# A 24-unit transformer kernel: each batch's recurrent layer moved inside the other batch's feed-forward unit, with the delta masks in the first unit

## The reference

```python
def ffn(x):                       # hidden size 1024
    return (silu(x @ w_gate.T) * (x @ w_up.T)) @ w_down.T

def recurrent(x):                 # RG-LRU
    xr, y = split(x @ W_xy.T)                         # 256 and 256 features
    xc = conv_b + sum(conv_w[i] * shift(xr, 3 - i) for i in range(4))
    gate_x = sigmoid(block_diag(xc, ig_w) + ig_b)
    log_a = -8 * sigmoid(block_diag(xc, ag_w) + ag_b) * softplus(a_param)
    a = exp(log_a)
    h = scan(a, xc * gate_x * sqrt(-expm1(2 * log_a)))    # h[t] = a[t] h[t-1] + in[t]
    return (gelu(y) * h) @ W_resid.T

x = x + 0.5 * ffn(layernorm(x))
x = x + recurrent(layernorm(x))
x = x + 0.5 * ffn(layernorm(x))           # the same weights again
x = x + 0.5 * moe1(layernorm(x))          # 8 experts; the weights of each are W plus a sparse delta
# moe1: weighted = softmax(expert_atom_weights) @ atoms * sigmoid(importance)  [8 x 2048],
#       added to W[e] at the 2048 places mask_idx (places that occur twice are summed)
...
```

## Time and profile before

| what | value |
|---|---|
| median of the runs | 1224.28 us (1220.64 to 1522.63, three runs) |
| the profiled execution, its span | 1237.2 us |
| granted clock of PE over the span | 0.969 |
| PE, DVE, ACT, POOL busy | 91 %, 67 %, 50 %, 45 % |

### The profile page before, as it was taken

How to read it: one execution, slowest core, us unless ns; L and a number is a source line. 1 busy time by engine, 2 the same in 40 slices (tenths; PEclk the granted TensorE clock), 3 DMA queues, 4 the chain that set the end, 5 groups by cost and what they waited for, 6 DMA issues and landing times.

```text
span 1237.2 us, 22024 instructions
## 1 busy us (share of the span) xinstructions
PE 1122.8 (91%) x6730; PEld 940.8 (76%) x6730; DVE 832.0 (67%) x2284; ACT 614.5 (50%) x1444; POOL 550.8 (45%) x662
## 2 busy tenths in 40 slices
PE   5887788999899989988889998998899998999997
PEld 4776457777677778877676777986799997899995
DVE  5477676778987855558867875556766665665666
ACT  2455745321122335457848756545455554555552
POOL 5466818743336443235524426323354442544431
PEclk9898799999989999999999999999999999999999
DMA  5125322230004023422102162343011110010101
GB/s 175 59 69 182 120 81 66 88 115 19 1 1 185 0 77 117 137 69 61 39 15 47 41 229 101 113 128 107 27 43 34 34 43 26 27 51 25 51 1 34
DMA packets 48468, 87.89 MB, mean 71 GB/s; under 512 B 9664, under 2 KB 28480, under 8 KB 47936
## 3 DMA queue, kind: packets, MB, share of 16 engines
q1 hardware_dynamic: 42400, 75.15, 19.2%
q0 software_dynamic: 3968, 8.85, 2.4%
q10 hardware_dynamic: 2016, 2.83, 0.7%
HBM read 61.24 MB, written 19.27 MB: 65 GB/s over the span
## 4 chain that ended last, share of the span: by engine, by line
PE 54%; DVE 19%; ACT 6%; issue 4%; POOL 2%; another core or an unknown queue 0%; SPq 0%; DMA 0%; DVEq 0%; POOLq 0%; ACTq 0%
PE ps L283 16%; PE ps L285 15%; PE ps L284 15%; DVE a_ptl L1898 4%; PE ps L1874 3%; DVE a_p L1833 2%; ACT a_pth L1890 2%; ACT a_p L1841 2%; PE ps L869 1%; DVE x L1587 1%; PE ps L888 1%; DVE stats L329 1%; DVE x L1050 1%; PE ps L1609 1%; PE ps L419 1%
## 5 line engine op out<-in xcount | busy, mean ns | idle before, releaser
L1859 POOL TENSOR_SCALAR a_p<-a_p,small 128x128 f32<-128x128 f32 (+3 forms) x256 | 132.7, 536 | 218.9 <-DVE small L1850 218.2
L1841 ACT ACTIVATE a_p<-a_p,small 128x128 f32<-128x128 f32 (+3 forms) x256 | 141.6, 554 | 79.2 <-DVE small L1833 77.5
L1898 DVE TENSOR_TENSOR a_ptl<-ps,a_pth 128x384 fp32r<-128x384 f32 (+1 forms) x192 | 106.7, 596 | 62.2 <-ACT a_pth L1890 62.0
L283 PE MATMUL ps<-xh,wh 128*128 128x512 f32 x304 | 124.9, 411 | 8.9 <-POOL wl L518 5.6
L284 PE MATMUL ps<-xl,wh 128*128 128x512 f32 x304 | 121.1, 398 | 0.0
L285 PE MATMUL ps<-xh,wl 128*128 128x512 f32 x304 | 121.0, 398 | 0.0
L1890 ACT ACTIVATE a_pth<-ps 128x384 fp32r<-128x384 f32 (+1 forms) x192 | 90.5, 523 | 59.5 <-PE ps L1874 58.9
L1833 DVE CUSTOM_DVE_ANT_0 a_p<-ps,maskrow 128x128 f32<-128x128 f32 (+3 forms) x256 | 111.7, 484 | 5.4 <-PE ps L285 2.5
L395 POOL TENSOR_TENSOR rstd<-veps,nhalf 128x4 f32<-128x4 f32 x24 | 26.0, 1085 | 182.6 <-DVE veps L339 182.6
L487 POOL TENSOR_TENSOR wl<-raw,wh 128x256 fp32r<-128x256 f32 (+1 forms) x64 | 89.0, 1390 | 5.3
L1874 PE MATMUL ps<-ident,a_p 128*128 128x128 f32 x640 | 84.9, 280 | 5.0 <-DVE a_kl L1898 2.1
(11 more groups left out here) (373 smaller groups left out, 3403.3 us busy)
## 6 DMA issues: line engine op xcount, KB each, us to landing
raw<-in_w SPq DMA_DIRECT2D x32, 384.0 KB
raw<-in_qk SPq DMA_DIRECT2D x16, 512.0 KB
raw<-moe_x SPq DMA_DIRECT2D x60, 128.0 KB
moe_y<-m_y SPq DMA_DIRECT2D x60, 128.0 KB
m_raw<-in_ex SPq DMA_DIRECT2D x8, 608.0 KB, 7.8
m_a<-in_ex SPq DMA_DIRECT2D x8, 608.0 KB, 5.4
raw<-in_v SPq DMA_DIRECT2D x16, 256.0 KB
moe_x<-drh SPq DMA_DIRECT2D x8, 480.0 KB
```

The source lines that it names most:

```text
L283: pe.matmul(o, l[0], r[0], start=start, stop=False, skip_group_check=True)
L1841: s.activation(p[:, par, P_AT[i]:P_AT[i + 1]], p[:, par, P_AT[i]:P_AT[i + 1]], ACT.Exp, bias=h_nmx[:, par, i:i + 1], scale=scale, accum_ou ...
L1859: g.tensor_scalar(pp, pp, h_inv[:, par, i:i + 1], 1.0, ALU.mult, ALU.mult).then_inc(sem("at_norm"), 1)
L1898: ins = v.tensor_tensor(dst, ps[:, bank, 0:cols], f32(hi), ALU.subtract)
```

## The change

The recurrent layer of batch 0 (unit 2) is worked off inside unit 1, that of batch 1 (unit 3) inside unit 4; the stage of its own is gone, and with it `pe_warm` in it. Its parts stand between the chunks: PE takes `rg_x`, `gates`, `y` and `out` between gate and up and down of the chunks 1 to 7, and the last two `down` stand behind `rg_out`; ACT and DVE take the rest, with the recurrent residual, and the statistics of the next unit, ahead of chunk 7. The recurrent weights come by ACT's queue in unit 0; ACT makes their high half, POOL their low half after the chunks 4 to 7. ACT's queue zeroes the delta table. The masks are all 2048 wide and there are no spare rows any more: 13 masks in unit 0, 3 in unit 1. Each of POOL's 16 scatters waits for the one before it to have landed; they stand between the chunks of units 1 and 4, and four of them ahead of unit 4's first splits. All four quarters stand in unit 5. The diff, cut:

```diff
-        DELTA_UNITS = (0, 1, 4, 5)
-        QUARTERS = ((4, 1), (4, 3), (4, 5), (5, 1))
-        EQ_SLOTS = [[0], [1, 2], [3, 4], [5, 6], [7, 8, 9], [10, 11, 12], [13, 14, 15]]
+        QUARTERS = ((5, 1), (5, 2), (5, 3), (5, 4))
+        EQ_MASK = {1: [0], 2: [1], 3: [2, 3], 4: [4, 5], 5: [6, 7, 8], 6: [9, 10], 7: [11, 12]}
+        EQ_SUM = {4: [0, 1, 2, 3], 5: [4, 5], 6: [6, 7, 8], 7: [9, 10]}
+        EQ_MASK_LATE = [13, 14], [15]
+        EQ_SUM_LATE = [11, 12, 13, 14, 15]
...
+        RG_OF = {1: 2, 4: 3}
...  pe_ffn
+            pe_ready(pe, u)
+            gate_up(0)
+            gate_up(1)
+            if u in RG_OF:
+                r = RG_OF[u]
+                if u == 1:
+                    pe_equal(pe, EQ_SUM_LATE)
+                down(0)
+                gate_up(2)
+                if u == 1:
+                    pe.wait_ge(sem("d_cmb"), 3)
+                pe_T(pe, r)
+                down(1)
+                pe_rg_x(pe, r)
+                gate_up(3)
+                down(2)
+                gate_up(4)
+                down(3)
+                pe_rg_gates(pe, r, 0)
+                gate_up(5)
+                down(4)
+                pe_rg_gates(pe, r, 1)
+                gate_up(6)
+                pe_rg_y(pe, r)
+                down(5)
+                gate_up(7)
+                pe_rg_out(pe, r)
+                down(6)
+                down(7)
+                pe_T(pe, 4 if u == 1 else 5)
...  dve_ffn
+            if u in RG_OF:
+                r, nxt = RG_OF[u], 4 if u == 1 else 5
+                if u == 1:
+                    dve_stats(v, r)
+                    chunk(0)
+                    dve_equal(v, EQ_MASK_LATE[0])
+                    chunk(1)
+                    dve_equal(v, EQ_MASK_LATE[1])
+                    dve_combined(v)
...
+                chunk(2)
+                dve_rg_pad(v, r)
+                dve_T(v, r)
+                dve_rg_conv(v, r, 0)
+                chunk(3)
+                dve_rg_conv_lo(v, r, 0)
+                dve_rg_conv(v, r, 1)
+                chunk(4)
+                dve_rg_conv_lo(v, r, 1)
+                chunk(5)
+                dve_rg_gate_input(v, r, 0)
+                dve_rg_gate_input(v, r, 1)
+                dve_rg_square(v, r, 0)
+                dve_rg_square(v, r, 1)
+                dve_rg_scan(v, r)
+                dve_rg_gated_lo(v, r)
+                chunk(6)
+                dve_residual(v, r, 1.0, [("rg_out", 2 * (r - 2) + 1), ("rg_out", 2 * (r - 2) + 2)], rg_o)
+                dve_stats(v, nxt)
+                chunk(7)
+                dve_residual(v, u, 0.5, ready)
+                dve_T(v, nxt)
+                dve_stats(v, 3 if u == 1 else 6)
...  act_delta
+            if u == 0 and j == 1:
+                s.dma_start(rg_wf[:, :], a["rglru"]).then_inc(sem("rg_w_in"), 16)
+            if u == 0 and 2 <= j <= 5:
+                act_zero(s, j - 2)
+            if u == 0 and 4 <= j <= 7:
+                act_rg_weights(s, j - 4)
...  pool_scatter
             for k in ks:
+                if k:
+                    g.wait_ge(sem("d_scattered"), 16 * k)
...  SP
-            sp_resident(sp, "rglru")
             sp_resident(sp, "wt")
-            sp_zero(sp)
             sp_zero_x(sp)
+            sp.dma_start(d_q3[:, :, :], a["weight3"]).then_inc(sem("d_in_q3"), 16)
             chunks(4)
...  POOL
+            for i in range(1, CH0 // 2):
+                for p in range(2):
+                    pool_chunks(g, 0, i, p)
+                    if i >= 2:
+                        pool_rg_weights(g, 2 * i + p - 4)
...
+            pool_resident(g, "wt")
+            pool_scatter(g, range(6, 10))
+            pre(4)
+            pool_ln(g, 4)
+            pool_ln(g, 3)
```

More of the change, by code:

```diff
@@ L314, in dr @@
             return drh[:, at:at + n], drl[:, at:at + n]
-        LN_AT = {u: u for u in range(N_UNITS)} | {20: 19, 19: 20}
+        LN_AT = {u: u for u in range(N_UNITS)} | {20: 19, 19: 20, 4: 3, 3: 4}
         def dve_stats(v, u, tiles=range(TT)):
@@ L634, in act_router, with gate_up @@
             s.activation(ex, dl, ACT.Exp).then_inc(sem("rt_exp"), 1)
-        def ffn_loop(eng, u, step, first, last):
-            n = CHUNKS[KIND[u]]
-            first()
-            if u in DELTA_UNITS:
-                for j in range(2, n - 2):
-                    step(j, j % 2)
-            else:
-                with eng.Fori(0, (n - 4) // 2) as i:
-                    for p in range(2):
-                        step(i * 2 + (2 + p), p)
-            last(n)
+        RG_OF = {1: 2, 4: 3}
         def pe_ffn(pe, u):
             b, f0, r0 = u % 2, FFN_AT[u], RAW0[u]
-            def gate_up(j, p, early=False):
+            def gate_up(j):
+                p = j % 2
                 pe.wait_ge(sem("w_gu"), f0 + 1 + j)
-                if not early:
+                if j >= 2:
                     pe.wait_ge(sem("ffn_silu"), f0 - 1 + j)
@@ new lines, in pe_rg_y, with pe_rg_out @@
+        def pe_rg_y(pe, r):
+            b = r - 2
+            for c in range(DC):
+                pe.wait_ge(sem("rg_sigm"), 4 * b + 2 + c + 1)
+                mm3c(pe, ps[:, c, :], [rc(k * 512 + (DC + c) * P, P) for k in range(DC)], [xT(b, k) for k in range(DC)])\
+                    .then_inc(sem("rg_xy"), 1)
+        def pe_rg_out(pe, r):
+            b = r - 2
+            pe.wait_ge(sem("rg_gelu"), DC * (b + 1))
+            pe.wait_ge(sem("rg_glo"), DC * (b + 1))
+            for t in range(TT):
+                last = mm3c(pe, rg_o(t), [(rg_ch[b][:, c, t * P:(t + 1) * P], rg_cl[b][:, c, t * P:(t + 1) * P])
+                                          for c in range(DC)], [rc(RG_WR + c * D, D) for c in range(DC)])
+                if t % 2:
+                    last.then_inc(sem("rg_out"), 1)
@@ new lines, in pe_rglru, with act_rg_x @@
+        def pe_rglru(pe, u):
+            return
+        def act_rg_x(s, r):
+            b = r - 2
+            s.wait_ge(sem("const_rgp"), 1)
+            s.wait_ge(sem("rg_pad"), b + 1)
+            for c in range(DC):
+                s.wait_ge(sem("rg_xy"), 4 * b + c + 1)
+                s.activation(rg_xp[b][:, c, 3:3 + T], ps[:, c, :], ACT.Copy).then_inc(sem("rg_x"), 1)
+                s.activation(rg_xc[b][:, c, :], ps[:, c, :], ACT.Identity, bias=rgp[:, c, 4:5], scale=rgp[:, c, 3:4])\
+                    .then_inc(sem("rg_tap"), 1)
@@ new lines, in act_rg_roots, with act_rg_gated_hi @@
+        def act_rg_roots(s, r):
+            b = r - 2
+            for c in range(DC):
+                s.wait_ge(sem("rg_m2"), DC * b + c + 1)
+                s.activation(rg_th[b][:, c, :], rg_th[b][:, c, :], ACT.Sqrt, scale=-1.0).then_inc(sem("rg_sqrt"), 1)
+        def act_rg_gated_hi(s, r):
+            b = r - 2
+            for c in range(DC):
+                s.wait_ge(sem("rg_g"), DC * b + c + 1)
+                s.activation(rg_ch[b][:, c, :], rg_gy[b][:, c, :], ACT.Copy).then_inc(sem("rg_ghi"), 1)
@@ new lines, in act_rglru, with dve_rg_pad, dve_rg_conv @@
+        def act_rglru(s, u):
+            return
+        def dve_rg_pad(v, r):
+            b = r - 2
+            v.wait_ge(sem("const_rgp"), 1)
+            if b == 0:
+                v.wait_ge(sem("d_zeroed"), 64)
+                v.wait_ge(sem("rg_wlo"), 4)
+            v.memset(rg_xp[b][:, :, 0:3], 0.0).then_inc(sem("rg_pad"), 1)
+            v.wait_ge(sem("rg_pad"), b + 1)
+        def dve_rg_conv(v, r, c):
+            b = r - 2
+            v.wait_ge(sem("rg_x"), DC * b + c + 1)
+            v.wait_ge(sem("rg_tap"), DC * b + c + 1)
+            for k in range(3):
+                if k:
+                    v.wait_ge(sem("rg_conv"), 6 * b + 3 * c + k)
+                v.scalar_tensor_tensor(out=rg_xc[b][:, c, :], in0=rg_xp[b][:, c, k:k + T], scalar=rgp[:, c, k:k + 1],
+                                       in1=rg_xc[b][:, c, :], op0=ALU.mult, op1=ALU.add).then_inc(sem("rg_conv"), 1)
@@ L2443, in pe_delta @@
                 last.then_inc(sem("d_delta"), 1)
-            if u == 1 and 1 <= j <= len(EQ_SLOTS):
-                o = ps[:, 0, 0:NK * 25].rearrange("p (m n) -> p m n", m=NK)
-                for k in EQ_SLOTS[j - 1]:
-                    pe.wait_ge(sem("d_eqs"), k + 1)
-                    for m in range(k, NK):
-                        last = pe.matmul(o[:, m, 0:24], d_eq[:, k % 3, m * P:(m + 1) * P], d_wb[:, k, 0:24],
-                                         start=(k == 0 and m == 0), stop=(k == NK - 1), skip_group_check=True)
-                    last.then_inc(sem("d_comb"), 1)
+            if u == 0 and j in EQ_SUM:
+                pe_equal(pe, EQ_SUM[j])
             if u == 5 and j == 6:
```

573 lines of the change are left out of this document (239 added, 334 removed).

## The result

The changed kernel takes 1260.06 us (median of 4 runs, 1259.02 to 1264.69) against 1222.46 us; the ratio is 1.0313, 95% interval [1.0279, 1.0347]: slower by some 38 us, where 17 were forecast. One of the four runs of before, of 1522.63 us, is left out of the ratio. The changed kernel's profiled execution has a span of 1258.3 us at a mean clock of 0.954.

The account below looks back on a forecast made before the run. The removed recurrent stage was taken as bound by waits on ACT and DVE. Units 0, 1, 4 and 5 at 70.7 + 75 + 68 + 48 = 261.7 against 245.1 gave +16.6 us, 1241; forecast 1229 to 1249, wider range 1206 to 1262.

Parts of the forecast that it names:

- the reference: Stages of units 0 to 5 in the first profile of before, 245.1 us; the difference was added to the median, 1224.3.
- the chain from `rg_x` to `rg_out`: Units 1 and 4: serial recurrent steps, mostly on ACT and DVE, with six table loads, 32.9 us in each unit.
- unit 1's tail: Unit 1 from `rg_out` to unit 4: `rg_out`, residual, statistics, chunk 7, last `down` and hand-off in series, 20.5 us.
- the start of `rg_x` in unit 4: Unit 4: `rg_x` comes at 14.7 us, as in unit 1 without masks, sums and one start at half clock.
- the price of nothing for four scatters: POOL ahead of unit 4's first splits: 9.7 us of scatters, beside unit 1's 20 us tail, costed at nothing.
- POOL's chain: Unit 0: POOL's split behind `rcl` sets chunk 4 to 5 (8.8 us) and 6 to 7 (8.0 us).
- unit 4's tail: Unit 4 from `rg_out` on, in series as in unit 1: 20.4 us.
- the half clock that the prediction adds there: Unit 0: `gate_up` behind long PE idle runs at half clock, 2.3 us added to each of two POOL chains.
- Rival 1: Units 0, 1, 4, 5: PE is the bound and waits are filled, 36 us less, 1188; chance in full 0.13.
- Rival 2: Units 0, 1, 4: half clock does not end, 16 to 20 us uncounted, 1257 to 1261; chance 0.22.
- Rival 4: Half the waits added in series fall together, 1209 to 1228; chance 0.17 together with half of rival 1.
- Rival 3: Chains in units 1 and 4: each table load also costs a drain of 1.38 us, 17 us more, 1258; chance 0.02.

Follow-up runs that it names:

- the run with the loads first: Changed kernel, recurrent weights' low halves out of unit 0, norm's pair of units 4 and 5 earlier, four unit 4 weight loads ahead of the zeroing: 1236.56 us, 1.0118.
- the run with the weights later: Changed kernel with the recurrent weights' low halves on POOL moved from unit 0's chunks to behind unit 2's layer norm in unit 1: 1254.18 us, 1.0270.
- The fillers: The run with the loads first plus 24 matmuls that compute nothing in PE's waits ahead of `rg_out` and the last `down`, units 1 and 4: 1235.89 us, 1.0113.
- narrow masks and mended queues: The run with the loads first, with masks 128 wide and one matmul of sums each: 1224.55 us, 1.0013 against the kernel before.
- the one with the quarters on POOL: The run with the loads first, with POOL instead of DVE making the low halves of unit 5's four quarters: 1234.61 us, 1.0125.

## Why the prediction was too small

The sign of the whole was right, the size was not: 17 us were forecast and 38 came. For units 1 and 4, the heart of the change, even the sign was wrong: the forecast took them to gain 11 us on the stages that they replace (143.0 against 154.3), and they lost 5. Of the 21 us between, the sum of the four stages was 14.8 too low and the reference 3.5 too high (245.1 against 241.7), which makes 34.9 by the stages; the other 2.7 of the 37.6 lie behind unit 5, where the profiles differ by more than that among themselves. The 14.8 are 6.7 of the chain from `rg_x` to `rg_out` in two units, 4.8 of unit 1's tail, 1.8 of the start of `rg_x` in unit 4 (16.5 for 14.7), 2.2 of unit 5, less 1.2 of unit 0, and 0.5 of the rest.

**The step that failed outright is the price of nothing for four scatters.** "The four ahead of unit 4's first splits take 4 × 2.4 = 9.7 us of POOL, beside the 20 us tail of unit 1 [...] so I cost them at nothing." They started at 140.3, only 10 us ahead of the time at which POOL was wanted, and took 14.1 us up to the end of the last, because each waited for a landing beside the 3.8 MB of zeros and the loads behind them. The tail took 25.3 us for 20.5 (the items given add up to 20.7), and 21.1 with the scatters out of the way: they cost 4.2 us of it. (The two other profiles that have scatters and norm's pair as the change put them show 25.0 and 24.3.) In the run with the loads first, where the scatters stand in the same place but the zeros come later and the norm's pair earlier, the tail from `rg_out` to unit 4 is 16.5 us (140.55 to 157.07), and with the weights later that run gives back 24 of the 38 us; the scatters alone, moved into unit 4, give nothing in all, for there PE waits 3.25 and 2.84 us for the splits behind them. The price of 2.4 us had come from a row without such a neighbour, and the neighbour stood in the diff.

**The chain from `rg_x` to `rg_out`** took 36.1 and 36.4 us for 32.9: over both units the largest term that was mis-sized. Its durations came from rows of the recurrent stage beside which POOL worked at the layer norm's small pair, at scatters or at nothing. Beside POOL's splits the same DVE steps are longer. In unit 1 (first three rows of the second block) the second convolution takes 3.38 where the first had 2.33, the scan pair 3.01 for 2.33, and the two products 1.95 for 1.26 (first block, of before); in unit 4 the convolution takes 3.38, the scan's inputs 2.17 for 1.28, and the scan pair 3.40.

```profile
161.41 1.26 DVE L1486 TENSOR_TENSOR rg_gy<-rg_gy,rg_xc 128x512 f32<-128x512 f32 x2
```

```profile
114.95 3.38 DVE L1504 SCALAR_TENSOR_TENSOR rg_xc<-rg_xp,rgp,rg_xc 128x512 f32<-128x512 f32 x3
...
135.83 3.01 DVE L1536 TENSOR_TENSOR_SCAN rg_xc<-rg_a,rg_xc 128x512 f32<-128x512 f32 x2
138.76 1.95 DVE L1541 TENSOR_TENSOR rg_gy<-rg_gy,rg_xc 128x512 f32<-128x512 f32 x2
...
192.82 3.38 DVE L1504 SCALAR_TENSOR_TENSOR rg_xc<-rg_xp,rgp,rg_xc 128x512 f32<-128x512 f32 x3
...
212.30 2.17 DVE L1532 TENSOR_TENSOR rg_xc<-rg_xc,rg_ga 128x512 f32<-128x512 f32 x2 [0.86 <-ACT rg_ga L1477]
214.39 3.40 DVE L1536 TENSOR_TENSOR_SCAN rg_xc<-rg_a,rg_xc 128x512 f32<-128x512 f32 x2
```

These steps are 2.4 us longer in unit 1 and 3.0 in unit 4, of the 3.2 and 3.5 by which the chain was too short. No run took the splits away from beside them. The prediction named this at its end as what would make it wrong, and put no price on it.

**Right:** unit 0 as a whole (70.7 forecast, 69.5 measured) with POOL's chain in it, which the run with the weights later confirms; the start of `rg_x` in unit 1 (21.6 and 21.8) and its wait of 6 to 8 us ahead of `rg_out` (6.92); unit 4's tail (20.4 and 20.7); unit 5 nearly (48.0 and 50.2), where the quarters add 9.5 us also in the kernel before. Inside unit 0 errors cancelled, which is luck: chunk 4's product came 30.8 us behind the start (32.1 forecast), the next three 8.7, 10.7 and 12.2 us behind each other (11.1, 10.7, 10.3), and the end took 7.1 (6.2). PE's wait ahead of chunk 5 was 2.7, not over 5, and the half clock that the prediction adds there didn't come (first row of the windows below), while it came at chunk 6, where none was added (second row). The row that it was read from, 52.26 of the earlier trace rows, doesn't stand behind a long idle time: PE had idled 1.79 us and then worked 5.8 us at 32 small matmuls of 8 columns:

```profile
43.83 5.78 PE L2441 MATMUL ps<-d_small,d_atoms 64*128 64x8 f32 x32 [1.79 <-DVE d_small L2513]
```

**The reference.** "The difference would change by 0.2 us" took the span's excess to be spread evenly. It lay for the most part behind unit 5, and 3.5 us of it in the stages that were compared. That under 2 per cent can hardly be told from none was too careful: the intervals of the ratios here are 0.2 to 0.5 per cent to either side.

**The rivals.** Rival 1 (the waits are filled) is out: PE waits 6.9 and 7.3 us ahead of `rg_out`. Rival 2 gave about the time that was measured (1257 to 1261) by a mechanism that the rows exclude: the granted clock is 1.00 over the whole chain in unit 1 up to the end of `gate_up(7)` (third row), and 1.00 from 184.06 to 213 in unit 4. It is low in the tails (last row, 0.59), where the prediction's sum has it. The fillers, which held the clock ahead of `rg_out`, changed nothing that can be measured, 1235.9 against 1236.6.

```profile
51.00:54.00 3.00, 2.90 (x12) 2.18 (x12) 2.97 (x6) 0.60 (x1) 2.25 (x3) 1.00 0.00 0
59.50:62.00 2.50, 2.47 (x6) 1.98 (x7) 2.26 (x10) 2.48 (x5) 1.08 (x2) 0.50 0.07 12
...
106.19:135.40 29.21, 28.67 (x144) 23.48 (x144) 18.51 (x22) 20.41 (x28) 20.18 (x22) 1.00 0.16 48
135.40:167.56 32.16, 12.05 (x56) 11.21 (x56) 15.56 (x32) 10.04 (x16) 15.93 (x18) 0.59 0.51 183
```

Rival 4 (half of the waits fall together, 1209 to 1228) is out by the time: unit 0 took what the sum in series gave, and unit 1's hand-off was longer than the sum has it. Rival 3 is out by the rows: the load of 1.28 us is followed by the next function 0.02 us later, so that the drain of the Trainium skill, "ScalarE: Activation LUTs", "What ACT_TABLE_LOAD costs", doesn't show here either. ACT's timeline in unit 1:

```profile
128.58 1.28 ACT L1469 ACT_TABLE_LOAD   x1
129.88 0.72 ACT L1469 ACTIVATE rg_a<-rg_ga,rgp 128x512 f32<-128x512 f32 x1
```

**What is left.** Of the 38 us, 24 are the queues' order on POOL and SP, with some 6 us of uncertainty; by differences of ratios, as estimates, some 5 are the weights' low halves, 12 the scatters and the norm's pair together, and 7 the loads ahead of the zeros. Of the 14 others the quarters' new place has 4 to 7, shown by that part alone; some 4 may be masks, which cost 12.8 us with the queues mended and 8.4 in before. The interleaved layer itself has brought no gain in any run: with narrow masks and mended queues units 1 and 4 take 144.1 us, and 143.3 with the recurrent stage in the kernel before, where unit 4 also holds three quarters (5.5 us). In that pair of runs unit 0 is 5.0 us longer and unit 5 8.0. How the last few us divide between the chain and unit 0 stays open: unit 0 took 59.2 to 64.5 us in five profiles of the same instructions, and their clock between 30 and 45 us differed too (0.64 in the run with the loads first, 0.89 in the one with the quarters on POOL).

## What to carry to other kernels

Work that is moved between the steps of another loop brings its waits along in every queue it passes: price it on the queue that stands behind it, with the slowest neighbour of that time (here a bulk of zeros on another queue, and POOL's splits beside DVE's chain), not with the row of a quiet stage. A serial chain hides only if the other work is not over first; PE had nothing left 7 us ahead of `rg_out`, and the hand-off to the next unit then lay bare behind it. And profile the kernel before twice where a difference of one or two per cent is to be sized.
